# First keys, first values and the start of the first attention of a two-layer cross-attention kernel: bias on TensorE, casts on ScalarE, a running maximum of the values, the first head's keys loaded in parts

## The reference

```python
kv = (cond @ Wkv + bkv).reshape(1, -1, 2, H, hd)   # cond: 12808 rows of 256; H = 16, hd = 16
k, v = (kv[:, :, 0], kv[:, :, 1])
q = _fq_sym(q, axis=-1)
k = _fq_sym(k, axis=-1)      # per key and head: s = max|k| / 127 (at least 1e-8), round(k / s) * s
v = _fq_sym(v, axis=2)       # per channel, over all 12808 keys
attn = jnp.einsum('bhqd,bhkd->bhqk', q, k)
attn = jax.nn.softmax(attn.astype(jnp.float32), axis=-1)
attn = _fq_unsigned(attn, axis=-1)
out = jnp.einsum('bhqk,bhkd->bhqd', attn, v)
```

## Time and profile before

| | us |
|---|---|
| Median of 3 runs | 7147.93 (7139.51 to 7154.99) |
| Profiled execution | 7151.02 |
| its span | 7149.2 |
| first keys: first matmul to next block's first operation | 148.9 to 551.9 |
| first values | 551.9 to 704.5 |
| wait before the first score | 704.5 to 734.5 |

### The profile page before, as it was taken

One profiled execution on the slowest core, in us unless ns is written; L12 is line 12 of the kernel. 1 busy time (PEld: TensorE's weight loads), 2 busy tenths in 40 slices (PEclk: granted clock), 3 DMA queues, 4 the chain that ended last, 5 costly groups with the idle time before them and its releaser, 6 DMA issues. The chain is left out here.

```text
span 7149.2 us, 180318 instructions
## 1 busy us (share of the span) xinstructions
PE 6052.2 (85%) x64319; PEld 2559.1 (36%) x64326; DVE 5668.0 (79%) x8927; ACT 4380.6 (61%) x4245; POOL 3730.7 (52%) x3972
## 2 busy tenths in 40 slices
PE   2761899999999999999999999999499667999623
PEld 2330133333333333333333333333355444544311
DVE  5885899999999999999999999999300346777655
ACT  0330089888898898888889888899000011666401
POOL 2331088888888888888888888888000001000000
PEclk7895599999999999999999999999688787999856
DMA  1432111001101101101100110110200058777500
GB/s 61 111 104 94 34 19 23 13 15 24 18 10 25 19 8 25 22 11 20 24 14 15 24 18 10 25 19 7 44 0 0 3 220 233 116 113 115 95 27 10
DMA packets 182696, 319.61 MB, mean 45 GB/s; under 512 B 97188, under 2 KB 143717, under 8 KB 176643
## 3 DMA queue, kind: packets, MB, share of 16 engines
q1 hardware_dynamic: 181784, 307.60, 20.2%
HBM read 196.26 MB, written 113.33 MB: 43 GB/s over the span
## 5 line engine op out<-in xcount | busy, mean ns | idle before, releaser
L1024 DVE TENSOR_REDUCE a_mx<-PS 128x1 f32<-128x512 f32 x6620 | 4073.0, 686 | 227.2 <-PE PS L908 223.6
L995 ACT ACTIVATE a_e<-PS,a_sk 126x1024 f32<-126x1024 f32 x3264 | 3630.2, 1113 | 459.2 <-PE PS L893 106.9
L771 POOL TENSOR_SCALAR a_p<-a_e 126x1024 f16<-126x1024 f32 x3264 | 3408.4, 1044 | 648.2 <-ACT a_e L995 596.1
L908 PE MATMUL PS<-a_K,a_Q 48*128 48x512 bf16 (+1 forms) x6884 | 2107.0, 383 | 49.9 <-DMA a_K<-d_inv 49.9
L893 PE MATMUL PS<-a_Q,a_K 54*126 54x512 bf16 x6528 | 2110.1, 404 | 27.7 <-issue 18.6
L935 PE MATMUL PS<-a_e,a_sel 126*32 126x256 f32 x26112 | 1992.8, 382 | 0.0
L893 PEld LDWEIGHTS PS<-a_Q,a_K 54*126 54x126 bf16 x6528 | 614.4, 131 | 1377.3 <-issue 1318.8
L931 PE MATMUL PS<-a_p,a_V 128*32 128x256 f16 x13056 | 959.6, 284 | 14.5 <-ACT a_og L976 10.5
L931 PEld LDWEIGHTS PS<-a_p,a_V 128*32 128x32 f16 x13056 | 336.7, 93 | 1250.2 <-POOL a_p L771 1054.2
L935 PEld LDWEIGHTS PS<-a_e,a_sel 126*32 126x32 f32 x26112 | 755.6, 110 | 8.5 <-issue 2.0
L1827 DVE TENSOR_REDUCE b_mx<-PS 128x1 f32<-128x512 f32 x803 | 504.7, 684 | 187.9 <-PE PS L1711 187.9
(11 more groups left out here) (288 smaller groups left out, 3717.1 us busy)
## 6 DMA issues: line engine op xcount, KB each, us to landing
b_K<-d_k SPq DMA_DIRECT2D x210, 200.1 KB, 6.0
a_K<-d_k SPq DMA_DIRECT2D x102, 400.2 KB
d_v<-v1v SPq DMA_DIRECT2D x9, 3328.0 KB, 11.5
b_V<-d_v SPq DMA_DIRECT2D x36, 832.0 KB, 12.0
d_k<-k_T SPq DMA_DIRECT2D x400, 63.0 KB, 1.7
d_k<-k1p SPq DMA_DIRECT2D x54, 400.2 KB, 7.6
a_V<-d_v SPq DMA_DIRECT2D x68, 204.0 KB, 2.8
d_v<-vq SPq DMA_DIRECT2D x17, 803.2 KB
```

The costliest lines, as they stand in the source:

```text
L771: g.tensor_scalar(p[0:rows, kk % RE, :], e[0:rows, kk % RE, :], 1.0, SHIFT, ALU.mult, ALU.add).then_inc(rounded, 1)
L908: last = pe.matmul(self.PS[:, M_BANK + j % sh.SLOTS, c0:c0 + wd], Qb[M_ROWS, ii % 4, t * P:(t + 1) * P], Kb[M_ROWS, (ii // NC) % 2, k0:k0 ...
L995: a.activation(e[0:r, kk % RE, :], self.PS[0:r, e_bank(i, s):e_bank(i, s) + 2, :], ACT.Exp, scale=skb[0:r, hb, s:s + 1]).then_inc(exp_done, 1)
L1024: v.tensor_reduce(mx[:, col:col + 1], bank, AX.X, ALU.max).then_inc(max_done, 1)
```

## The change

In `first_keys` the bias is added on PE: VectorE splits it once into three bf16 rows (0, 32 and 64 of `bp`), and a bf16 matmul with `pick`, ones in those three rows, closes each product. Keys and values of a group now lie in banks of their own, as products of 256 columns. VectorE reads the keys from PSUM twice (maximum, scaling). ScalarE makes HI and MID, copies the values to `v_raw` and their magnitudes to `v_abs`; VectorE keeps a running maximum in `v_top`. The steps are skewed: `rest` and `last` of a group stand in the next group's place, transposes and stores two groups behind the matmuls. The turned parts are copied two kinds at a time. In `first_values` the fold over partitions is done with two transposes, a reduction, two diagonals and a matmul with ones in place of L566 and L607; scaling is by halves; each head is passed on when it is rounded. In `first_attention` the first head's three maximum parts are loaded in five stretches of keys, and the first pass waits by stretch.

```diff
+                        store(g - 2)
+                store(NG - 2)
...
+                pe.wait_ge(zeroed, 11)
+                pe.wait_ge(bias_ready, 3)
...
+                        pe.wait_ge(kv_seen, g - 1)
+                        pe.wait_ge(v_taken, g - 1)
+                    for y in range(2):
+                        for j, n in tiles(g):
+                            kv = self.PS[0:n, 2 * (g % 2) + y, j * D:(j + 1) * D]
+                            for c in range(2):
+                                pe.matmul(kv, cT[:, g % RC, c, j * KT:j * KT + n], W[:, c, y * D:(y + 1) * D],
+                                          start=(c == 0), stop=False)
+                            last = pe.matmul(kv, pick[0:96, 0:n], bp[0:96, y * D:(y + 1) * D], start=False, stop=True)
                     last.then_inc(kv_ready, 1)
-                    if g >= 1:
-                        turn(g - 1)
+                    if g >= 2:
+                        turn(g - 2)
+                turn(NG - 2)
...
+                g.memset(pick[:, :], 0.0).then_inc(zeroed, 1)
+                g.wait_ge(zeroed, 1)
+                for i in range(3):
+                    g.memset(pick[32 * i:32 * i + 1, :], 1.0).then_inc(zeroed, 1)
+                    g.wait_ge(zeroed, 2 + i)
                 g.memset(self.v_raw[:, NKT - 1, :], 0.0).then_inc(zeroed, 1)
-                g.wait_ge(zeroed, 1)
+                g.memset(self.v_top[:, :, :], 0.0).then_inc(zeroed, 1)
...
+                by_head = lambda ap: ap.rearrange("p t (h d) -> p t h d", d=HD)
+                v.wait_ge(zeroed, 11)
                 v.wait_ge(ld_w, 32)
-                for g in range(NG):
+                self.link(v, v.tensor_copy(bp[:, :], bkv[:, :]), self.dv)
+                self.link(v, v.tensor_tensor(bt[:, 0, :], bkv[:, :], bp[:, :], ALU.subtract), self.dv)
+                self.link(v, v.tensor_copy(bm[:, :], bt[:, 0, :]), self.dv)
+                self.link(v, v.tensor_tensor(bt[:, 1, :], bt[:, 0, :], bm[:, :], ALU.subtract), self.dv)
+                v.tensor_copy(bp[32:64, :], bm[32:64, :]).then_inc(bias_ready, 1)
+                v.tensor_copy(bp[64:96, :], bt[64:96, 1, :]).then_inc(bias_ready, 1)
+                v.wait_ge(bias_ready, 2)
+                v.sem_inc(bias_ready, 1)
+                def scales(g):
                     b = g % 2
                     v.wait_ge(kv_ready, g + 1)
-                    tl = tiles(g)
-                    rows = [(slice(0, GT), KT)] if all(n == KT for _, n in tl) else [(slice(j, j + 1), n) for j, n in tl]
-                    for s, n in rows:
-                        ps = self.PS[0:n, 2 * b + s.start:2 * b + s.stop, :]
-                        nt = s.stop - s.start
-                        self.link(v, v.tensor_tensor(kf[0:n, b, s, :], ps[:, :, 0:D],
-                                                     along(bkv[0:n, 0:D], 1, nt), ALU.add), self.dv)
-                        self.link(v, v.tensor_tensor(self.v_raw[0:n, g * GT + s.start:g * GT + s.stop, :], ps[:, :, D:2 * D],
-                                                     along(bkv[0:n, D:2 * D], 1, nt), ALU.add), self.dv)
-                    v.sem_inc(kv_taken, 1)
+                    if g >= 2:
+                        v.wait_ge(ip_ready, g - 1)
+                    for s, n in spans(g):
+                        ps = self.PS[0:n, 2 * b, :].rearrange("p (t d) -> p t d", d=D)[:, s, :]
+                        sc = sk[0:n, :, g * GT + s.start:g * GT + s.stop].rearrange("p h t -> p t h")
+                        rc = rk[0:n, b, s, :]
+                        self.link(v, v.tensor_reduce(sc, by_head(ps), AX.X, ALU.max, apply_absolute_value=True), self.dv)
+                        self.link(v, v.tensor_scalar(sc, sc, 1.0 / 127.0, 1e-8, ALU.mult, ALU.max), self.dv)
+                        self.link(v, v.reciprocal(rc, sc), self.dv)
+                        if s.stop == GT:
+                            v.sem_inc(rk_ready, 1)
+                        self.link(v, v.tensor_tensor(by_head(tmp[0:n, b, s, :]), by_head(ps), along(rc, 3, HD), ALU.mult), self.dv)
+                    v.sem_inc(kv_seen, 1)
+                def rest(g):
...
+                    v.wait_ge(cast, 2 * g + 1)
+                    for s, n in spans(g):
+                        self.link(v, v.tensor_tensor(tmp2[0:n, b, s, :], kf[0:n, b, s, :], parts[0:n, b, HI, s, :], ALU.subtract), self.dv)
+                    v.sem_inc(to_cast, 1)
...
+                def largest(g):
+                    v.wait_ge(v_taken, g + 1)
+                    for s, n in spans(g):
+                        top = self.v_top[0:n, s, :]
+                        self.link(v, v.tensor_tensor(top, v_abs[0:n, g % 2, s, :], top, ALU.max), self.dv)
...
+                def last(g):
+                    b = g % 2
+                    v.wait_ge(cast, 2 * g + 2)
+                    for s, n in spans(g):
+                        self.link(v, v.tensor_tensor(parts[0:n, b, LO, s, :], tmp2[0:n, b, s, :], parts[0:n, b, MID, s, :], ALU.subtract), self.dv)
+                    v.sem_inc(parts_ready, 1)
...
+                for g in range(NG):
+                    scales(g)
+                    if g >= 1:
+                        rest(g - 1)
+                    whole(g)
+                    if g >= 1:
+                        last(g - 1)
+                    scaled(g)
+                    largest(g)
+                rest(NG - 1)
+                last(NG - 1)
...
+                def high(g):
+                    a.wait_ge(to_cast, 2 * g + 1)
+                    a.activation(parts[0:KT, g % 2, HI, :, :], kf[0:KT, g % 2, :, :], ACT.Copy).then_inc(cast, 1)
+                def middle(g):
+                    a.wait_ge(to_cast, 2 * g + 2)
+                    for s, n in spans(g):
+                        ins = a.activation(parts[0:n, g % 2, MID, s, :], tmp2[0:n, g % 2, s, :], ACT.Copy)
+                    ins.then_inc(cast, 1)
+                def values(g):
+                    a.wait_ge(kv_ready, g + 1)
+                    if g >= 2:
+                        a.wait_ge(kv_seen, g)
+                    for s, n in spans(g):
+                        ps = self.PS[0:n, 2 * (g % 2) + 1, :].rearrange("p (t d) -> p t d", d=D)[:, s, :]
+                        a.activation(self.v_raw[0:n, g * GT + s.start:g * GT + s.stop, :], ps, ACT.Copy)
+                        ins = a.activation(v_abs[0:n, g % 2, s, :], ps, ACT.Abs)
+                    ins.then_inc(v_taken, 1)
...
+                    for i in range(2):
+                        a.activation(kT[:, g % 2, 2 * i:2 * i + 2, :, :].rearrange("p i c n -> p (i c n)"),
+                                     self.PS[:, 4 + i, :].bitcast(BF16)[:, 0:4 * GW], ACT.Copy).then_inc(self.ac, 1)
+                    a.activation(iT[:, g % 2, :], self.PS[0:HEADS * IROWS, 6, :].bitcast(BF16)[:, 0:GW], ACT.Copy).then_inc(self.ac, 1)
+                    self.count[id(self.ac)] += 3
...
+                a.wait_ge(zeroed, 11)
+                for g in range(NG):
+                    if g >= 3:
+                        evacuate(g - 3)
+                    if g >= 1:
+                        high(g - 1)
+                    values(g)
+                    if g >= 1:
+                        middle(g - 1)
+                evacuate(NG - 3)
+                high(NG - 1)
+                middle(NG - 1)
+                evacuate(NG - 2)
+                evacuate(NG - 1)
...
-                L(v.tensor_reduce(mx[:, :], self.v_raw[:, :, :].rearrange("p t d -> p d t"), AX.X, ALU.max,
-                                  apply_absolute_value=True))
-                v.sem_inc(part_max, 1)
+                L(v.tensor_tensor(self.v_top[:, 0, :], self.v_top[:, 0, :], self.v_top[:, 1, :], ALU.max))
+                v.sem_inc(top_ready, 1)
                 L(v.memset(cs[:, :, :], 0.0))
-                L(v.tensor_copy(ident[:, :], self.idf[:, :]))
+                v.wait_ge(top_turned, 1)
+                L(v.tensor_reduce(top[:, :], self.PS[:, 2, 0:2 * P].rearrange("p (c k) -> p c k", c=2)[:, :, 0:KT], AX.X, ALU.max))
+                for c in range(2):
+                    L(v.tensor_scalar(spread[:, c, :], self.idf[:, :], top[:, c:c + 1], None, ALU.mult))
+                v.sem_inc(spread_ready, 1)
...
+                L(v.tensor_scalar(amx[:, :], self.PS[:, 3, 0:D], 1.0 / 127.0, 1e-8, ALU.mult, ALU.max))
                 v.sem_inc(scaled, 1)
                 L(v.reciprocal(rv[:, :], amx[:, :]))
-                L(v.tensor_tensor(self.v_raw[:, :, :], self.v_raw[:, :, :], along(rv[:, :], 1, NKT), ALU.mult))
                 for c in range(2):
+                    w = slice(c * P, (c + 1) * P)
+                    L(v.tensor_tensor(self.v_raw[:, :, w], self.v_raw[:, :, w], along(rv[:, w], 1, NKT), ALU.mult))
                     v.wait_ge(zeroed, 2)
-                    if c == 1:
-                        v.wait_ge(stored, 16 * 9)
-                        v.wait_ge(summed, 1)
                     for h in range(8):
+                        if c == 1:
```

(32 more changed lines are left out.)

116 lines of the change are left out of this document (55 added, 61 removed).

## The result

The changed kernel took 7041.3 us (median of 4 runs, 7034.0 to 7045.1) where the kernel before took 7151.5 (7139.5 to 7155.5): a ratio of 0.9847, 95% interval 0.983 to 0.9865, or 110 us less. Forecast were 7029 us in a range of 6998 to 7056. The profiled execution took 7040.7 us. The table sets it beside the one of before, stage by stage.

A forecast was written before the change was run, and what follows sets the result against it. The prediction took VectorE to bound the key loop, a serial chain the first values, and the last key load the attention's start. Its terms, -46 - 51 - 22 = -119 us, gave 7029 us, range 6998 to 7056.

The forecast's parts named there:

- Term 1: First keys' loop: VectorE's period falls from 7.46 to 6.4 us a group; with the ends, -46 us (-56 to -23).
- the new wait: Key loop: VectorE's low-part subtraction waits for ScalarE's middle cast, 0.2 us a group remaining, bounds 0 and 0.4.
- The ends: Start and end of the first keys' block: added clearings, bias splitting, slower first matmuls and a longer tail, +8 us.
- Term 2: First values: reduction and all-reduce removed, scaling by halves, heads passed on when rounded; -51 us chosen.
- the hold: First values: VectorE's spread operation cannot run until POOL's clearing of vq ends at 21.9 us; gives -51 us.
- the forecast's other end: First values: the spread runs beside POOL's clearing, so the block takes 84 us in place of 152.6, -68 us.
- Term 3: First attention's start: PE begins on parts of the keys, 8.1 us in, behind POOL's clearing; -22 us.
- Nothing behind the attention's start changes: Everything after PE's first attention score: the forecast claimed no change in time there.
- rival 1: First values: the spread is not held by POOL's clearing; 17 us less, 7012 us; chance 0.32.
- rival 2: Key loop: ScalarE or PE takes over, period 6.85 to 7.2 us; +23 to +40, 7052 to 7070 us; chance 0.08.
- rival 3: Key loop: PE loses its clock and the kernel gets slower, 7243 us at half clock throughout; chance 0.02.
- rival 4: Attention's start: the key stretches come late, gaining only 8 us, 7043 us in all; chance 0.05.

The follow-up runs named there:

- The experiment with two tensors: Changed kernel, the values' two spread diagonals made from two SBUF tensors, not one with a scalar: 7010.5 us, ratio 0.9813 to the kernel before.

## Why the prediction was right, and where it was not

1. **Term 1, the loop:** busy 5.16 forecast, 5.18 measured; the new wait 0.2 forecast, 0.25 measured. Gaps were over-priced: period less busy, less the wait, is 6.27 - 5.18 - 0.25 = 0.84 us, where I took 1.0. With these the parts add up to 6.27, where the forecast's gave 6.36, rounded to 6.4; 51 times 0.13 is 6.6 us. The ends cost +5.8 in place of +8 (-54.9 + 60.7). Together these are the 9 us between -46 and -54.9. PE had more slack than thought, for its clock rose to full speed. (The forecast's upper sum for ScalarE, 5.9 us, comes out at 5.7 from its own rows; nothing hangs on it. ScalarE was busy 4.3.)
2. **Term 2, the values:** -49.9 against -51, with the hold as chosen (19.33 us). The experiment with two tensors prices the hold at 17.8 us (17 forecast); without it the values took 67.7 us less than before, the forecast's other end, -68.
3. **Term 3, the start:** -21.9 against -22, behind POOL as forecast.
4. **"Nothing behind the attention's start changes" failed.** It was two things. The all-reduce that term 2 removed had a second cost at the end of the first pass: -7.0 us. And the 1237 added PE instructions moved the attention's loop in the instruction stream: +28.7 us, shown by taking it away in the changed kernel and by putting it into the kernel before. The forecast counted what instructions take and never where they lie. The time stayed in its range partly by luck: the first three terms overshot by 8, the all-reduce gave 7, and the part behind the attention, which no term covers, 6.
5. **The rivals:** the spread was held (against rival 1); neither ScalarE nor PE took the loop (rival 2), even with VectorE's share cut further; the clock went up in the key loop (rival 3); the stretches were not late (rival 4).

## What to carry to other kernels

Where a loop jumps back on an engine, look at the "issue" idle time of its first lines before and after an edit, even one far ahead of the loop: here instructions added before the loop cost 29 us, and 20 useless transposes in idle time took 19 to 24 of them away again. Read such a gain in the loop and not in the total, which moved by 10 to 20 us for reasons of its own. Beside a long POOL clearing, use forms of VectorE with two inputs from SBUF for the small operations on the path; here a cast and a scalar form waited for the clearing's end. When an operation of a rare kind is removed, look for its second cost at the next ordinary operation of that engine.

## What the runs showed of the hardware that was not expected

- PE stalls at the loop's jump back in every build: 2.4 to 3.5 us where no second stall follows, 3.5 to 4.5 where one does. The second stall, 3.5 to 5.2 us, comes some 15 to 25 instructions behind the first where the loop lies in certain places of the instruction stream: there for +0, +8 and +256 instructions, not for +40 and +128.
- Behind a `partition_all_reduce` POOL's next arithmetic operation starts 7.1 to 7.3 us behind its releaser in place of 0.2, even 198 and 265 us later and with clearings in between.
- A 128-partition cast of 512 columns that takes 0.43 us alone took 18.39 us beside a clearing, and two tensor_scalar operations of 128 columns took 19.33 us; a tensor_tensor operation is not held by the same clearings.
- Kernels with the same instructions behind the attention spent 2119 to 2149 us there; VectorE's busy time is the same, PE's differs with its granted clock (half clock for 769 to 834 us of that part).
